# A fused Perceiver layer on one core: another order for the first groups of the cross-attention

## The reference

```python
x = x + xattn(layernorm(x), ctx, ctx, Wq, bq, Wk, bk, Wv, bv)   # 257 keys of 256 for each batch
    # q = Q Wq^T + bq ; k = K Wk^T + bk ; v = V Wv^T + bv ; softmax(q k^T) v
x = x + attn(layernorm(x), Wq, Wk, Wv, Wo, W_feat)              # causal linear attention, 16 heads of 64
    # phi(u) = exp(u W_feat - |u|^2/2)/sqrt(128); v = x Wv; y = causal sum / (denominator + 1e-6); y Wo
x = x + ffn(layernorm(x), w1, w2)                               # quantised activations and weights, exact gelu
```

## Time and profile before

| | us |
|---|---|
| median of 3 runs | 252.69 |
| lowest and highest | 252.28, 252.93 |
| the profiled execution's own time | 252.84 |
| its span, first to last instruction | 251.0 |

### The profile page before, as it was taken

The page is one execution under the profiler, slowest core; times in us unless marked ns, Lnnn a source line. Parts: engine busy times, 40 slices in busy tenths (PEclk is TensorE's granted clock), DMA queues, the critical chain, the costliest instruction groups (busy, mean ns, idle before and its releaser), DMA issues.

```text
span 251.0 us, 7011 instructions
## 1 busy us (share of the span) xinstructions
PE 240.3 (96%) x2736; PEld 189.2 (75%) x2736; DVE 187.2 (75%) x474; ACT 146.6 (58%) x285; POOL 101.6 (40%) x139
## 2 busy tenths in 40 slices
PE   8998889999999999999999999999999999999985
PEld 7854557777687778777777787777788988888845
DVE  5677888666733585867888888775578999999985
ACT  0553453544445788567556666755747257787772
POOL 2073113342202558443673568727530034444430
PEclk9999999999999999999999999999999999999999
DMA  6999999991079001100110000000000000000002
GB/s 179 367 384 404 396 396 394 340 393 45 1 224 331 33 0 46 44 3 1 44 44 3 1 3 3 3 0 3 4 3 3 4 0 3 21 21 24 22 24 65
DMA packets 15521, 26.83 MB, mean 107 GB/s; under 512 B 1248, under 2 KB 8832, under 8 KB 15488
## 3 DMA queue, kind: packets, MB, share of 16 engines
q1 hardware_dynamic: 14720, 25.96, 29.1%
q10 hardware_dynamic: 768, 0.43, 0.6%
HBM read 25.33 MB, written 1.05 MB: 105 GB/s over the span
## 4 chain that ended last, share of the span: by engine, by line
PE 62%; DVE 14%; DMA 5%; SPq 5%; POOL 5%; issue 4%; ACT 4%; DVEq 0%; POOLq 0%; ACTq 0%
PE b L1364 11%; PE b L1124 8%; PE b L1126 7%; PE b L1125 7%; PE b L1408 6%; DMA wv_raw<-in_aWv 5%; PE b L1383 4%; PE b L1285 3%; PE b L1288 2%; PE b L1495 2%; PE b L1281 2%; SPq L270 2%; PE b L1536 2%; SPq L276 2%; DVE yT_lo L996 1%
## 5 line engine op out<-in xcount | busy, mean ns | idle before, releaser
L868 DVE TENSOR_TENSOR x_lo<-b,x_hi 128x512 fp32r<-128x512 f32 x32 | 21.7, 688 | 16.8 <-ACT x_hi L472 16.7
L609 ACT ACTIVATE phi<-b 128x512 f32<-128x512 f32 x48 | 26.0, 597 | 11.3 <-PE b L1364 11.3
L354 POOL TENSOR_TENSOR lnr<-lnv,mh 128x1 f32<-128x1 f32 x16 | 8.8, 551 | 55.6 <-DVE lnv L732 55.6
L412 POOL TENSOR_TENSOR sq_lo<-sq_sum,sq_hi 128x512 fp32r<-128x512 f32 x16 | 20.6, 1286 | 25.8 <-ACT sq_hi L472 25.8
L530 ACT ACTIVATE sq<-b 128x512 f32<-128x512 f32 x32 | 19.3, 603 | 18.2 <-PE b L1126 18.2
L406 POOL TENSOR_TENSOR sq_sum<-sq,sq 128x512 f32<-128x512 f32 x16 | 20.7, 1294 | 21.7 <-ACT sq L530 21.7
L1124 PE MATMUL b<-nT_lo,wp_hi 128*128 128x512 f32 x64 | 26.8, 419 | 0.1
L1126 PE MATMUL b<-nT_hi,wp_hi 128*128 128x512 f32 x64 | 25.1, 392 | 0.0
L1125 PE MATMUL b<-nT_hi,wp_lo 128*128 128x512 f32 x64 | 25.0, 391 | 0.0
L942 DVE TENSOR_TENSOR smk<-b,mask 64x512 f32<-64x512 f32 x32 | 22.0, 688 | 2.9 <-PE b L1383 1.2
L1408 PEld LDWEIGHTS b<-va,smk 128*64 128x64 f32 x512 | 17.5, 137 | 7.4 <-issue 7.0
(11 more groups left out here) (181 smaller groups left out, 617.9 us busy)
## 6 DMA issues: line engine op xcount, KB each, us to landing
cT<-in_ctxT SPq DMA_DIRECT2D x8, 1028.0 KB, 14.2
cn<-in_ctx SPq DMA_DIRECT2D x8, 1024.0 KB, 14.9
wv_raw<-in_aWv SPq DMA_DIRECT2D x1, 1024.0 KB, 13.7
wp_raw<-in_aWq SPq DMA_DIRECT2D x4, 256.0 KB, 4.7
wp_raw<-in_aWk SPq DMA_DIRECT2D x4, 256.0 KB, 4.7
w_raw<-in_w2T SPq DMA_DIRECT2D x1, 1024.0 KB, 5.6
wo<-in_aWo SPq DMA_DIRECT2D x1, 1024.0 KB, 8.1
w_raw<-in_w1T SPq DMA_DIRECT2D x1, 1024.0 KB, 5.0
```

The source lines that it names most:

```text
L412: nc.gpsimd.tensor_tensor(sq_lo[n % 2][:], sq_sum[:], sq_hi[n % 2][:].bitcast(F32), ALU.subtract).then_inc(sq_l, 1)
L609: nc.scalar.activation(phi(n, a)[:], feature_bank(a), ACT.Exp).then_inc(f_exp, 1)
L868: nc.vector.tensor_tensor(x_lo[n % 2][r][:], proj_bank(n, r), x_hi[n % 2][r][:].bitcast(F32), ALU.subtract).then_inc(x_l, 1)
```

## The change

Loads: xWk is issued first instead of x of groups 0 and 1. The rest of x comes as groups 2 and 3, 4 and 5, and 6 and 7 (four transfers in all, three before), and groups 6 and 7 come after group 2's `cn`. Wv comes in two halves with a semaphore each, around group 2's `cT`. The broadcast bias bv is issued by SyncE instead of ScalarE.

ScalarE loads its table ahead of the 257th keys' transfers, by a copy of two columns. GpSimd does `x_rstd(2)` before the first `add_bias`, and `add_bias(2)` with `add_bias(3)`, behind the first group's new x.

The loop's first three rounds are written out by hand on each of TensorE, VectorE and ScalarE, and from i = 3 the loop goes on. `qk(2)` (groups 4 and 5), `nT(1)` and both halves of `values(0)` now stand ahead of `scores(3)`; before, `scores(3)` stood ahead of all of them but `values(0, 0)`.

```diff
@@ sync
+            load_weight(xwk, xWk, ld_m)
             load_x(0, 0, 2)
-            load_weight(xwk, xWk, ld_m)
...
             load_weight(xwv, xWvT, ld_xwv)
+            load_x(2, 4, 6)
             load_cT(1)
-            load_x(2, 4, NG)
+            sp.dma_start(bvb[:], bv.rearrange("(a d) -> a d", a=1).broadcast_to([P, D])).then_inc(ld_bv, 16)
             load_cn(1)
+            load_wv(0)
             load_cT(2)
-            load_weight(wv_raw, aWv, ld_wv)
+            load_wv(1)
             load_cn(2)
+            load_x(3, 6, NG)
@@ gpsimd
-            for g in range(3):
+            x_rstd(2)
+            for g in range(2):
                 add_bias(g)
-            x_rstd(2)
...
                 if g == 0:
+                    add_bias(2)
                     add_bias(3)
@@ scalar
+            act.wait_ge(setup_dve, 1)
+            copy(spare[:], mh[:, 0:2])
...
-            act.dma_start(bvb[:], bv.rearrange("(a d) -> a d", a=1).broadcast_to([P, D])).then_inc(ld_bv, 16)
...
+            avT(1)
+            split_wv(0)
+            nT(0)
+            qk(2)
+            exp(2)
+            pTc(2)
+            split_wv(1)
+            vcopy(0, 0)
+            nT(1)
+            vcopy(0, 1)
+            for i in range(3, NG + 1):
+                avT(i - 1)
...
+                if i == 3:
+                    vcopy(1, 0)
                 if i < NG:
                     exp(i)
@@ vector
             stats(0, 0, 2)
+            dve.wait_ge(m_h, 1)
+            nc.vector.tensor_tensor(m_lo[:], b4.rearrange("p (c d) -> p c d", c=DC), m_hi[:].bitcast(F32),
+                                    ALU.subtract).then_inc(m_l, 1)
             x_norm(0)
             x_norm(1)
...
+            def residual(g):
+                settle()
+                x1(g)
+                dve.wait_ge(x1_cp, g + 1)
+                stats(1, g, g + 1)
...
+            for i in range(3, NG + 1):
                 if i < NG:
                     softmax_bias(i)
+                avT(i - 1)
...
                 if i < NG:
                     inverse_sum(i)
+                residual(i - 1)
+                x2_norm(i - 1)
                 if i == 3 or i == 5:
                     t_bias((i + 1) // 2)
@@ tensor
-            xT(0)
             bias_v1()
             bias_u()
+            xT(0)
             qk(0)
...
+            for i in range(3, NG + 1):
                 if i < NG:
                     scores(i)
...
+                avTt(i - 1)
+                if i == 3:
+                    values(1, 0)
+                if i >= 4:
                     nT(i - 2)
                     values(i - 3, 1)
+                wv(i - 1)
```

More of the change, by code:

```diff
@@ L778, in _ @@
                                   ).then_inc(cl_sel, 1)
[L779 to L782 removed]
+            dve.wait_ge(v1_mm, 1)
+            nc.vector.tensor_copy(v1b[:], b3[:, 0:D + 2]).then_inc(v1_cp, 1)
             dve.wait_ge(u_mm, 1)
@@ L879, in split_wv_low @@
                                         ALU.subtract).then_inc(wv_l, 1)
-            for i in range(NG + 1):
-                if i == 2:
-                    avT(i - 1)
+            def residual(g):
[3 more added lines that the diff above has]
+                stats(1, g, g + 1)
+            softmax_bias(0)
+            x_norm(2)
+            x_norm(3)
+            inverse_sum(0)
+            xT(1)
+            avc(0)
+            dve.wait_ge(ld_x[2], 16)
@@ new lines, in _ @@
+            stats(0, 4, 6)
+            softmax_bias(1)
+            avT(0)
+            x_norm(4)
+            x_norm(5)
+            inverse_sum(1)
+            residual(0)
+            avc(1)
+            x2_norm(0)
+            xT(2)
+            t_bias(1)
+            avT(1)
+            split_wv_low(0, 0)
+            split_wv_low(0, 1)
+            nT(0)
+            softmax_bias(2)
+            residual(1)
+            inverse_sum(2)
+            x2_norm(1)
+            split_wv_low(1, 0)
@@ L884, in _ @@
+            split_wv_low(1, 1)
+            nT(1)
+            avc(2)
+            dve.wait_ge(ld_x[3], 16)
+            stats(0, 6, 8)
+            for i in range(3, NG + 1):
                 if i < NG:
                     softmax_bias(i)
-                if 0 <= i - 1 and i != 2:
-                    avT(i - 1)
-                if 0 <= i - 2:
+                avT(i - 1)
+                if i >= 4:
                     nT(i - 2)
-                if i == 0:
-                    x_norm(2)
-                    x_norm(3)
@@ L1303, in project @@
                     mm.then_inc(a_mm, 1)
-            xT(0)
             bias_v1()
             bias_u()
+            xT(0)
             qk(0)
             pe.wait_ge(u_cp, 1)
-            for i in range(NG + 1):
+            scores(0)
+            last_keys(0)
+            last_keys(1)
+            pTt(0)
+            xT(1)
+            avm(0)
+            qk(1)
+            scores(1)
+            avTt(0)
+            last_keys(2)
+            wv(0)
+            pTt(1)
+            xT(2)
+            avm(1)
+            last_keys(3)
+            avTt(1)
+            qk(2)
+            nT(0)
+            wv(1)
+            scores(2)
+            values(0, 0)
+            pTt(2)
+            avm(2)
+            nT(1)
+            values(0, 1)
+            for i in range(3, NG + 1):
                 if i < NG:
                     scores(i)
-                if i == 0:
-                    last_keys(0)
-                    last_keys(1)
                 if i == NG:
```

110 lines of the change are left out of this document (35 added, 75 removed).

## The result

The changed kernel takes 255.25 us (median of 4 executions, 254.95 to 255.47) against 252.70: ratio 1.0102, 95% interval 1.0086 to 1.0118. It is slower, as forecast, by 2.55 us where 1.15 were forecast, and outside the range (252.1 to 254.7). The profiled execution has a span of 253.3 us, 2.3 more than before.

A forecast was written before the change was run, and what follows sets the result against it. VectorE's chain to avTt(3), not TensorE, was taken to set the end: start +0.6, scores(3) 1.7 behind its context, -0.55 behind it, +1.15 in all; 252.69 + 1.15 = 253.8 us, range 252.1 to 254.7.

The forecast's parts named there:

- The frame: Orders match from avTt(3) on, so whatever avTt(3) moves, the whole time moves by as much; 1.15 us later forecast.
- Rival 1: At scores(3): the chain catches up and it again starts when its context lands; 252.1, in part to 253.1; chance 0.27.
- rival 2: Work moved ahead of scores(3) pays in full: avTt(3) 2 to 2.9 us earlier, 249.8 to 250.7; chance 0.10.
- Rival 3: ScalarE's table load delays m_hi to 8.5, chain 0.9 us later, 254.7; chance 0.13 together with another late link.
- step 1: Start of the kernel: the new order makes scores(0) and scores(1) 0.6 us later, scores(1) at 18.97.
- step 2: From scores(1) to scores(3): a chain through all engines puts scores(3) at 34.6, 1.7 us after its context lands.
- step 3: From scores(3) to x1(2): 4.05 us instead of 4.60, so x1(2) at 38.65 against 37.48.
- the forecast's low end of 253.1: Lower end of the main forecast's 253.1 to 254.4, said to come from the bounds of t_bias(1) and the start.
- the four signs named for being wrong: qk(0) before 10.4; scores(3) waiting for context; x1(2) under 3.8 behind it; avTt(3) and the end moving by different amounts.
- the bound of 0.8: Upper bound on how many us later the start makes scores(0) and what follows; the lower bound was 0.
- the disputed price: VectorE's t_bias(1) beside GpSimd's bias additions: 1.8 us taken, with 1.07 and 2.17 as the ends.
- the edits that cost nothing: Late loads of groups 6 and 7, x_rstd(2) ahead of add_bias(0), bv's new queue, SyncE's three more issues: no cost.

The follow-up runs named there:

- run 4: Changed kernel with t_bias(2) and t_bias(3) on VectorE behind avc(3) and avc(5) instead of ahead of them: 254.77 us, ratio 1.0083.
- run 8: Changed kernel with the edits of experiment 1, run 2, run 3 and run 4 together: 252.13 us, ratio 0.9977.
- run 11: Kernel of run 8 with GpSimd's additions of bv for groups 4 to 7 one round later as well: 251.04 us, ratio 0.9949.
- experiment 1: Changed kernel, start put back: x of groups 0 and 1 before xWk, xT(0) before bias products, m_lo behind two normalisations: 253.93 us, ratio 1.0065.
- Experiment 9: Changed kernel with only the first two loads put back (x of groups 0 and 1 ahead of xWk): executions of 255.71 and 257.14 us.
- run 2: Changed kernel with GpSimd's order put back (three bias additions before x_rstd(2), one behind the first x2_norm): 253.90, 254.31, 256.29, 256.51 us.
- run 7: Changed kernel without GpSimd's eight additions of bv, so the output lacks the bias of the values: 253.96 us.
- run 5: The changed kernel measured once more, unchanged: executions of 254.91, 255.33, 255.66, 257.02 and 257.11 us.
- run 3: Changed kernel with exp(3) on ScalarE ahead of the copy of values(1, 0): executions of 254.73, 254.78, 256.76 and 256.99 us.

## Why the prediction was right in sign and too small

**The frame held.** `avTt(3)` moved by 2.25 us and the span by 2.3: what happens up to `avTt(3)` is carried to the end one for one in this pair. (It is not a rule: in runs 4, 8 and 11 the order behind `avTt(3)` differs, and part of the gain is lost by `avTt(4)`.) From `x1(2)` to `avTt(3)` it is 4.94 us after the change, as before (4.95). `scores(3)` waits for VectorE and ScalarE and not for its context; TensorE stands idle for 2.20 us ahead of `avTt(3)`. Rival 1 (the chain catches up) and rival 2 (the moved work pays) did not come about; experiments 1 and 4 show why: a late start passes through undiminished, and the moved work goes into the wait. Rival 3, the dearer table load, is not seen: 2.25 to 3.53, the next activation at 3.55. Of what the Trainium skill (ScalarE: Activation LUTs, "What ACT_TABLE_LOAD costs") gives, the load agrees with this trace too (1.28 us), and the drain is not to be seen in the new place either.

**What failed is the size of the terms.** The steps that were put too small are step 1, the start (0.60 us, measured 1.02), and in steps 2 and 3 three links of the chain (together 0.70); no term was put too long by more than 0.03:

| link | forecast, us | measured, us | difference |
|---|---|---|---|
| start: `scores(1)` later than 18.37 by | 0.60 | 1.02 | 0.42 |
| `scores(1)` to `t_bias(1)` | 6.20 | 6.52 | 0.32 |
| `t_bias(1)` | 1.80 | 1.77 | -0.03 |
| end of `t_bias(1)` to `scores(3)` | 7.63 | 7.90 | 0.27 |
| `scores(3)` to `x1(2)` | 4.05 | 4.16 | 0.11 |

Together 1.09, and with the 1.15 forecast the 2.25 of the trace. The measured column is of one execution, and the start varies by some tenths between executions (run 1); from `scores(1)` to `scores(3)` it is 16.16 to 16.20 us in all eight profiles that have the changed order there. The medians are 2.55 apart, 0.3 more than the profiled executions; that part is within what the executions of either kernel differ by. One sum of the prediction is off as well, on the side that did not matter: the forecast's low end of 253.1 takes the 1.07 of `t_bias(1)` but not the bound of 0 for the start, with which it would be 252.5. And none of the four signs named for being wrong looked for a term that is too small.

Step 1, the start, is the term that was missed most, and its measured value lies beyond the bound of 0.8 that I gave. M started at 5.40 as forecast and the normalisations ended at 9.65 (9.6 forecast); behind them the transposes and their copy took 1.4 us and not 1.2, and `qk(0)` to `scores(0)` took 1.89 us and not the 1.61 of before, because `xT_lo` now comes later than its first products need it: I had put 0.1 for that. Experiment 9 shows that the order on the engines is the cause, as the step said, and experiment 1 that all of it reaches `avTt(3)`.

Step 2 got the disputed price right: `t_bias(1)` beside GpSimd 1.77 us for 1.8, and experiments 2 and 7 show that GpSimd's additions make it. What it overlooked is the same effect in a place where it had not been in the trace of before: GpSimd's first two additions moved behind `x_rstd(2)` and so beside `softmax_bias(1)`, whose last small addition went from 0.16 to 0.63 us. `avT(0)` and `wv(0)` waited for it, a path through VectorE where the sum had TensorE's own work. I had counted `x_rstd(2)` ahead of `add_bias(0)` among the edits that cost nothing; with GpSimd's old order (run 2) this link is 6.19 us, so it makes the whole 0.32. That 6.20 was forecast for it is in part luck: `last_keys` takes 0.64 instead of 0.86 us there and `wv(0)` 0.94 instead of 0.71, and the two errors cancel.

The remaining 0.4 us lie in three places; the other links of this stretch (`softmax_bias(2)` to `exp(2)`, to `pTc(2)`, to the copy of Wv's second half, to its split) came out within 0.03. `scores(2)` starts 0.91 us behind the end of `t_bias(1)`, not 0.7, and `softmax_bias(2)` then waits for it, 1.14 us behind it at 29.73: 0.12 late. From the start of the split at 33.10 to `scores(3)` it is 2.48 us and not 2.35. And the copy of `values(1, 0)` starts 2.87 us behind `scores(3)`, where I had it start together with `wv(2)` at 2.75. All three lie where TensorE starts up behind another engine or another engine behind TensorE; they were put too short or left out, all in one direction, and the range did not allow for them. The rule of the Trainium skill (SBUF — State Buffer, "Who interferes with whom") was applied to the instruction that I looked at and not to all instructions with two inputs in SBUF on the chain; the addition of 128x1 at 0.63 us agrees with it.

## What to carry to other kernels

Moving work ahead of a wait gives time only if the wait that then ends last is for that work; here it was for VectorE's list, in which two microseconds of `t_bias` stood in front of what TensorE waited for, and putting that list right together with the start, `exp(3)` and GpSimd's additions (runs 8 and 11) turned 1% slower into 0.5% faster. When a chain over several engines is added up from rows, add the bounds on the long side of every link and check each VectorE instruction on it, the smallest too, for what GpSimd does at that moment; an edit that moves all of it by a microsecond can bring other instructions together, as in run 8. A wait of the bound engine can cost more than its length: in four profiles the work behind it took 1.5 us longer at the lower clock.

## What the runs showed of the hardware

A GpSimd addition of 128x256 in SBUF lengthens VectorE instructions with two inputs in SBUF that fall beside it: a 128x1 addition from 0.16 to 0.63 us, a dot product of 256 columns from 0.42 to 0.95. With the additions left out both are back at 0.16 and 0.42 (run 7), and so are those that no addition falls beside in runs 2 and 11. The small one and the large one lose about the same half microsecond. Not every instruction beside an addition is lengthened (0.16 at 20.99 after the change), and not only those with two inputs: the addition of a constant to a 128x2 tile in SBUF goes from 0.17 to 0.47 (run 2) and 0.71 us (run 8).

Behind a wait of 2.2 us TensorE's granted clock was at 0.66 to 0.78 from 45 to 50 us in four of six profiled executions (runs 1, 2, 5 and 9), and the way from `avTt(3)` to `avTt(4)` took 8.14 to 8.21 us there instead of 6.64. In the two others (after the change, and run 3 with a wait of 2.38 us) it stayed at 1.00. Filled with products of ones the same place showed 1.00 in both profiles. That the wait is what lowers the clock is likely but not shown. A second such place is the start: in the profiles of runs 2, 5 and 7, behind 0.69 us of idle time ahead of `qk(0)` and the lighter work before it, the clock was at 0.50 from 12 to 14 us, and in run 7 it took 9.7 us from `qk(0)` to `scores(1)` instead of 8.3.
